# A weight stream refilled in halves of the ring: 8 MB transfers in place of 2 MB ones

## The chip, the cores and the metric

One core of a Trainium2 chip. The metric is the device time of one execution in microseconds; lower is better. All data are float32.

## The reference

The input is one image of 16 channels and 64 x 64 pixels. Four layers follow each other:

- L0 normalises the image with a 13 x 13 Gaussian blur (mean and standard deviation of the image and of a style image) and rescales it.
- L1 is a two-stage attention layer. Patches of 8 x 8 x 16 = 1024 values (64 of them) go through `Wqk_p` (1024 x 2048), `Wv_p` (1024 x 1024), attention inside each of four windows, a depthwise convolution and `Wout_p` (1024 x 1024). The four windows of 32 x 32 x 16 = 16384 values go through `Wqk_w` (1024 x 2048, on pooled values), `Wv_w` (16384 x 1024), attention between the windows, and `Wout_w` (1024 x 16384). Both results are added to the image.
- L2 is two 3 x 3 convolutions of 16 channels with a ReLU between them.
- L3 is L1 again with weights of its own.

What matters for the time: each attention layer reads 24 MB of smaller matrices (8 + 4 + 8 + 4 MB), then 64 MB of `Wv_w`, then 64 MB of `Wout_w` (MB here is 1024 x 1024 bytes). Each weight is used once, so 304 MB are read per execution.

## The kernel before

The weights are laid out as one `stream` in the order of use. The unit of use is a slot of 1 MB (2048 float32 in each of 128 partitions). The stream is read in pairs of slots (`PAIR`), that is in transfers of 2 MB with a contiguous row of 16 KB for each partition, into `ring`, which has eight such buffers (`RING`), 16 MB in all. There are 152 buffers' worth, and the last one is split into two transfers of 1 MB, so the SyncE queue (SP) issues 153 transfers for the ring.

SP issues them in order. It loads the images and the constants first (L227, L228), then eight ring buffers (L231). From then on it waits, before the transfer into buffer k, until TensorE has used the two slots that lay in it (`slots_free`, which waits on `slots_used`), and issues it (L238, L241; L244 and L245 for the two last).

TensorE (PE) runs the matmuls in one fixed order and adds one to `slots_used` after each slot. Before the first slot of a pair it waits for the pair's landing (`landed`). Its stages in each attention layer, with their lines: `Wqk_p` 8 slots (L341), `Wv_p` 4 slots (L350), turns of q, k and v (L259), `Wqk_w` 8 slots (L358) with the scores between them (L377), `Wout_p` 4 slots (L407), `Wv_w` 64 slots (L429), a short chain over ScalarE (ACT) and VectorE (DVE), and `Wout_w` 64 slots (L452). A slot is four matmuls of 512 columns for the last two stages; each shows as two instructions, so a slot is 8 instructions there. `Wout_w` is worked in groups of 8 slots (`GROUP`); after each group ACT copies the result (L579), PE turns it (L259) and DVE adds it to the image (L847). After the last group but one the finished rows are turned (L492) and stored (L594), the residual of the last rows is put into the accumulator (L499), and then the last group of 8 slots runs, whose last slot waits for the last 1 MB transfer. DVE copies the result (L868) and SP stores it (L248).

ACT fills `stage` (L567) for each 8 slots of `Wv_w`, once the 8 slots before are used. The first layer's arrays `l0_in`, `l0_sq` and `l0_blur` have memory of their own; `image_turned` is set when PE has read the last of them (L304).

Of the kernel before, what the change touches and what calls it, by code (L numbers as in the profile page):

```python
# [17 lines left out]
F32 = mybir.dt.float32  # L18
# [4 lines left out]
P = 128  # L23
# [10 lines left out]
SLOT = 2048  # L34
RING = 8
PAIR = 2
BANK = 512
# [13 lines left out]
PER_LAYER = S_OUTW + N_OUTW  # L51
TURNS = N_VW // (RING * PAIR)
GROUP = PD // P
N_BUFFERS = 2 * PER_LAYER // PAIR
assert TURNS * RING * PAIR == N_VW == N_OUTW and RING * PAIR == 2 * GROUP and N_BUFFERS % RING == 0

# [47 lines left out]

def build(nc, images, const, window_gains, small, l2w, stream, out, windows_last):
    with ExitStack() as ctx:
        def sb(name, *shape):
            return ctx.enter_context(nc.sbuf_tensor(name, list(shape), F32))

        def sem(name):  # L110
            return ctx.enter_context(nc.semaphore(name))


        ring = sb("ring", P, RING, PAIR * SLOT)
        cst = sb("cst", P, N_CONST)
# [48 lines left out]
        gains_landed, small_landed = sem("gains_landed"), sem("small_landed")  # L164
        ring_landed = [sem(f"ring_landed{i}") for i in range(RING)]
        slots_used = sem("slots_used")
        last_landed = sem("last_landed")
        last_stored = sem("last_stored")
# [30 lines left out]

        l0_in = ctx.enter_context(nc.sbuf_tensor("l0_in", [P, C, IMG], F32))  # L200
        l0_sq = ctx.enter_context(nc.sbuf_tensor("l0_sq", [P, C, IMG], F32))
        l0_blur = ctx.enter_context(nc.sbuf_tensor("l0_blur", [P, 2, 2 * BANK], F32))

        out_rows = l0_in[0:IMG].rearrange("y c x -> y (c x)")
        l0_part = l0_sq[:, :, :].rearrange("p c x -> p (c x)").rearrange("p (s n) -> p s n", s=2)

        def slot_of(L, s):

            buffer, half = divmod(L * PER_LAYER + s, PAIR)
            return ring[:, buffer % RING, half * SLOT:(half + 1) * SLOT], ring_landed[buffer % RING], buffer // RING  # L210

        def used(L, s):

            return L * PER_LAYER + s
# [10 lines left out]
        @block.sync  # L225
        def _(sp):
            sp.dma_start(l0_in[:, :, :], images).then_inc(images_landed, 16)  # L227
            sp.dma_start(cst[:, :], const).then_inc(const_landed, 16)  # L228

            for k in range(RING):  # L230
                sp.dma_start(ring[:, k, :], stream[k]).then_inc(ring_landed[k], 16)  # L231
            def slots_free(t, k):
                sp.wait_ge(slots_used, t * (RING * PAIR) + ((k + 1) * PAIR - RING * PAIR))

            with sp.Fori(1, N_BUFFERS // RING - 1) as t:
                for k in range(RING):
                    slots_free(t, k)
                    sp.dma_start(ring[:, k, :], stream[t * RING + k]).then_inc(ring_landed[k], 16)  # L238
            for k in range(RING - 1):
                slots_free(N_BUFFERS // RING - 1, k)  # L240
                sp.dma_start(ring[:, k, :], stream[N_BUFFERS - RING + k]).then_inc(ring_landed[k], 16)  # L241

            slots_free(N_BUFFERS // RING - 1, RING - 1)
            sp.dma_start(ring[:, RING - 1, 0:SLOT], stream[N_BUFFERS - 1][:, 0:SLOT]).then_inc(ring_landed[RING - 1], 16)  # L244
            sp.dma_start(ring[:, RING - 1, SLOT:], stream[N_BUFFERS - 1][:, SLOT:]).then_inc(last_landed, 16)  # L245
# [8 lines left out]
        def _(pe):  # L254
# [5 lines left out]

            def landed(L, s, turns=0):
                _, semaphore, fills = slot_of(L, s)
                if s % PAIR == 0:
                    pe.wait_ge(semaphore, turns * 16 + 16 * (fills + 1))

# [43 lines left out]
            for L in range(2):  # L309
# [26 lines left out]
                for s in range(S_QKP, S_VP):  # L336
                    landed(L, s)
                    w = slot_of(L, s)[0].rearrange("p (m h b d) -> p m b h d", m=2, b=2, d=P)
                    for m2 in range(2):
                        for b in range(2):  # L340
                            m = mm(bank[4 + m2][b * 64:b * 64 + 64, :], fl[:, s - S_QKP, :], w[:, m2, b], start=(s == S_QKP), stop=(s == S_VP - 1))  # L341
                    m.then_inc(slots_used, 1)

                for s in range(S_VP, S_QKW):
                    landed(L, s)
                    w = slot_of(L, s)[0].rearrange("p (t h b d) -> p t b h d", t=2, b=2, d=P)
                    for t in range(2):
                        kt = 2 * (s - S_VP) + t
                        for b in range(2):
                            m = mm(bank[6][b * 64:b * 64 + 64, :], fl[:, kt, :], w[:, t, b], start=(kt == 0), stop=(kt == KT - 1))  # L350
                    m.then_inc(slots_used, 1)

                def qk_of_windows(lo, hi):
                    for s in range(lo, hi):
                        landed(L, s)
                        w = slot_of(L, s)[0]
# [44 lines left out]
                for s in range(S_OUTP, S_VW):  # L401
                    landed(L, s)
                    w = slot_of(L, s)[0].rearrange("p (t f n) -> p t f n", t=2, f=2)
# [17 lines left out]
                with pe.Fori(0, TURNS) as i:  # L421
                    for k in range(RING * PAIR):
                        if k % 8 == 0:
                            pe.wait_ge(staged, i * 2 + (2 * TURNS * L + k // 8 + 1))
                        landed(L, S_VW + k, i)
                        w = slot_of(L, S_VW + k)[0].rearrange("p (j n) -> p j n", j=4)
# [17 lines left out]
                def group(i, g, onto=None):  # L444
                    for h in range(GROUP):
                        k = g * GROUP + h
                        landed(L, S_OUTW + k, i)
                        if onto is not None and h == GROUP - 1:
                            pe.wait_ge(last_landed, 16)
                        w = slot_of(L, S_OUTW + k)[0].rearrange("p (j n) -> p j n", j=4)  # L450
# [53 lines left out]
        def _(act):  # L504
# [25 lines left out]
            for L in range(2):  # L530
# [32 lines left out]
                with act.Fori(0, TURNS) as i:  # L563
                    for half in range(2):

                        act.wait_ge(slots_used, i * (RING * PAIR) + (used(L, S_VW) + 8 * half - 8))
                        sc.copy(stage[:, half, :], area[2][:, bass.ds(i * 128 + 64 * half, 64)]).then_inc(staged, 1)  # L567
# [7 lines left out]
                def copy_group(i, g):  # L575
                    act.wait_ge(slots_used, i * (RING * PAIR) + used(L, S_OUTW + GROUP * (g + 1)))
# [338 lines left out]
```

## Time and profile before

| | |
|---|---|
| time, median of 3 runs | 762.57 us (761.68 to 762.76) |
| span of the profiled execution | 760.3 us |
| outside of that span, against the median | 2.3 us |
| bytes moved in the profiled execution | 320.82 MB (10^6 bytes), 422 GB/s over the span |
| transfers into the ring | 151 of 2 MB and 2 of 1 MB |
| PE busy | 499.3 us (66%) |
| DVE busy, ACT busy | 92.3 us (12%), 38.0 us (5%) |

The profile is one execution. Its span is counted from the first to the last instruction; the time of that execution itself is not given apart from the three runs, so the 2.3 us between span and median are taken as what lies around it. Busy time of an engine is the time in which it works, and the DMA share is the mean busy share of the 16 DMA engines. In the timeline, a transfer shows through what waits for it: a PE row with "<-DMA ring<-stream" starts when a transfer has landed.

### The profile page before, as it was taken

Reading aid. Unit: us, or ns where it says so; the run is one execution under the profiler, and the core shown is the slowest. Engines: PE = TensorE matmul, PEld = TensorE weight load, DVE = VectorE, ACT = ScalarE, POOL = GpSimd, SP = SyncE. Lnnn points to the kernel's source line nnn. Section 1 sums busy time; section 2 is a strip of 40 time slices with the busy share of each in tenths; the row PEclk is TensorE's granted clock in tenths of the full one; section 3 lists DMA queues with packets and bytes.
Section 4 is the critical chain, followed back from the end, with each engine's and each line's share of the span. In section 5 each row is a group of like instructions: output and inputs, shape, how many; then the busy total and the mean of one; then the engine's idle time right before and its main releaser. Section 6 shows DMA issues by size and latency. Waiting matters only on the chain.

```text
span 760.3 us, 7405 instructions
## 1 busy us (share of the span) xinstructions
PE 499.3 (66%) x3076; PEld 143.4 (19%) x3076; DVE 92.3 (12%) x254; ACT 38.0 (5%) x79; POOL 8.8 (1%) x19
## 2 busy tenths in 40 slices
PE   6599675556556656565677979565665576666565
PEld 5234210000002211121122433000000121111121
DVE  3754400000001000000006071000000100000000
ACT  2111100000000000000001010000000000000000
POOL 2100000000000000000001000000000000000000
PEclk9589898786878777878897989978677877768789
DMA  9999999999999999999999999999999999999996
GB/s 367 427 391 431 427 428 428 429 428 428 428 428 429 428 428 428 428 428 429 428 428 427 424 428 427 431 428 428 428 428 428 428 428 428 428 430 428 429 428 280
DMA packets 22856, 320.82 MB, mean 422 GB/s; under 512 B 2569, under 2 KB 2689, under 8 KB 3257
## 3 DMA queue, kind: packets, MB, share of 16 engines
q1 hardware_dynamic: 22464, 320.04, 99.1%
q10 hardware_dynamic: 377, 0.56, 0.2%
q8 instruction: 12, 0.20, 0.1%
q14 instruction: 3, 0.02, 0.0%
HBM read 320.10 MB, written 0.49 MB: 422 GB/s over the span
## 4 chain that ended last, share of the span: by engine, by line
DMA 72%; PE 20%; DVE 6%; issue 1%; ACT 1%; SPq 0%; DVEq 0%; ACTq 0%
DMA ring<-stream 71%; PE bank L341 4%; PE bank L452 3%; PE bank L429 3%; PE bank L407 2%; DVE conv_p L772 2%; PE bank L350 2%; PE bank L259 1%; DMA cst<-const 1%; PE bank L358 1%; PE bank L476 1%; PE bank L270 0%; DVE l_sq L644 0%; PE bank L312 0%; PE bank L474 0%
## 5 line engine op out<-in xcount | busy, mean ns | idle before, releaser
L452 PE MATMUL bank<-ring,wf_t 128*32 128x512 f32 x1024 | 169.3, 797 | 99.1 <-DMA ring<-stream 93.7
L429 PE MATMUL bank<-ring,stage 128*4 128x512 f32 x1024 | 162.3, 773 | 107.5 <-DMA ring<-stream 107.5
L452 PEld LDWEIGHTS bank<-ring,wf_t 128*32 128x32 f32 x1024 | 32.7, 131 | 215.3 <-DMA ring<-stream 147.8
L429 PEld LDWEIGHTS bank<-ring,stage 128*4 128x4 f32 x1024 | 24.7, 94 | 243.3 <-DMA ring<-stream 163.6
L259 PE MATMUL bank<-cst,area 128*128 128x128 f32 (+1 forms) x234 | 38.5, 318 | 15.3 <-ACT area L579 11.6
L259 PEld LDWEIGHTS bank<-cst,area 128*128 128x128 f32 (+1 forms) x234 | 32.9, 219 | 43.9 <-ACT area L579 33.8
L847 DVE TENSOR_TENSOR image<-bank,image 128x32 f32 (+1 forms) x30 | 5.1, 194 | 278.3 <-PE bank L259 278.3
L341 PE MATMUL bank<-ring,area 128*64 128x512 f32 x128 | 33.7, 692 | 1.7 <-DVE area L728 1.7
L821 DVE COPY wv_t<-bank 128x32 f32<-128x32 f32 x2 | 0.4, 192 | 275.4 <-PE bank L259 275.4
L579 ACT COPY area<-bank 128x512 f32<-128x512 f32 x15 | 8.8, 586 | 282.3 <-PE bank L452 282.3
L407 PE MATMUL bank<-ring,area 128*64 128x512 f32 x64 | 18.0, 727 | 0.0
L341 PEld LDWEIGHTS bank<-ring,area 128*64 128x64 f32 x128 | 10.2, 159 | 24.4 <-issue 21.7
L358 PE MATMUL bank<-ring,pooled_n 128*32 128x512 f32 x128 | 14.6, 595 | 0.0
L772 DVE SCALAR_TENSOR_TENSOR conv_p<-v_pad,vec,conv_p 128x636 f32<-128x636 f32 x16 | 14.1, 881 | 0.6
L567 ACT COPY stage<-area 128x64 f32 x16 | 3.9, 242 | 205.6 <-PE bank L429 192.5
L350 PE MATMUL bank<-ring,area 128*64 128x512 f32 x64 | 14.1, 592 | 0.0
L270 PE MATMUL bank<-cst,l_in 128*128 128x128 f32 x16 | 3.7, 422 | 6.8 <-DMA cst<-const 6.8
L407 PEld LDWEIGHTS bank<-ring,area 128*64 128x64 f32 x64 | 5.3, 169 | 11.1 <-issue 11.0
L398 PE MATMUL bank<-wqk_t 128*32 128x32 f32 x4 | 0.6, 251 | 10.2 <-DVE wqk_t L787 10.2
L612 POOL TENSOR_TENSOR area<-area,vec 128x512 f32<-128x512 f32 x2 | 2.1, 1042 | 395.6 <-DVE area L703 395.6
L350 PEld LDWEIGHTS bank<-ring,area 128*64 128x64 f32 x64 | 4.5, 137 | 9.2 <-issue 9.2
L304 PE MATMUL bank<-cst,l_blur 128*64 128x64 f32 x32 | 2.0, 317 | 6.3 <-DVE l_blur L652 6.3
(193 smaller groups left out, 196.4 us busy)
## 6 DMA issues: line engine op xcount, KB each, us to landing
ring<-stream SPq DMA_DIRECT2D x151, 2048.0 KB, 35.5
ring<-stream SPq DMA_DIRECT2D x2, 1024.0 KB, 35.8
l_in<-images SPq DMA_DIRECT2D x1, 512.0 KB, 4.4
cst<-const SPq DMA_DIRECT2D x1, 461.0 KB, 5.6
area<-window_gains ACTq DMA_DIRECT2D x1, 256.0 KB, 4.6
windows_last<-area SPq DMA_DIRECT2D x1, 256.0 KB, 2.0
out<-l_in ACTq DMA_DIRECT2D x2, 112.0 KB
area<-small ACTq DMA_DIRECT2D x1, 52.0 KB
```

The lines of the kernel that those rows point to most:

```text
L259: return mm(dst, src, ident[0:rows, 0:rows], start=True, stop=True)
L341: m = mm(bank[4 + m2][b * 64:b * 64 + 64, :], fl[:, s - S_QKP, :], w[:, m2, b], start=(s == S_QKP), stop=(s == S_VP - 1))
L350: m = mm(bank[6][b * 64:b * 64 + 64, :], fl[:, kt, :], w[:, t, b], start=(kt == 0), stop=(kt == KT - 1))
L358: m = mm(bank[7][32 * j:32 * j + 32, :], pooled_n[:, s - S_QKW, :], w[:, j * BANK:(j + 1) * BANK], start=(s == S_QKW), stop=(s == S_OUTP - 1))
L407: m = mm(bank[4][f * 64:f * 64 + 64, :], a3(8, TOK)[:, h, :], w[:, t, f], start=(h == 0), stop=(h == HEADS - 1))
L429: m = mm(bank[0][32 * j:32 * j + 4, :], stage[:, k // 8, at:at + 4], w[:, j], start=False, stop=False)
L452: m = mm(bank[6 + g][32 * j:32 * j + 32, :], wf_t[:, h, :], w[:, j], start=(h == 0 and onto is None), stop=(h == GROUP - 1))
L476: mm(dst[0:32, :], taps_edge[:, n, dy, 0, :], rows(dy, -1), start=False, stop=False)
L567: sc.copy(stage[:, half, :], area[2][:, bass.ds(i * 128 + 64 * half, 64)]).then_inc(staged, 1)
L579: sc.copy(area[4 + g][:, :], bank[6 + g][:, :]).then_inc(group_copied, 1)
L772: then(v.scalar_tensor_tensor(conv_p[:, 0:159, 0:4], src, wt, conv_p[:, 0:159, 0:4], ALU.mult, ALU.add))
L847: m = v.tensor_tensor(dst, grp[:, 2 * wy:2 * wy + 2], dst, ALU.add)
```

## The change

The ring keeps its 16 MB but is filled in two halves of 8 slots, each by one transfer of 8 MB with a row of 64 KB for each partition. The weights come as two arrays, `quarters` (the 24 MB of smaller matrices of each layer, in transfers of 4 MB with rows of 32 KB) and `halves` (`Wv_w` and `Wout_w`). A further buffer `extra` of 4 MB (32 KB for each partition) takes the first and the last of a layer's six quarters; the other four go into the ring. The arrays of the first layer lie in the ring's last quarter, which is therefore filled only after `image_turned`. The halves at a layer's start and at the very end are cut: the first half of a layer comes as two transfers of 4 MB, and the last 8 slots of the kernel as 4, 2, 1 and 1 slots (`LAST_CUTS`).

```diff
-        ring = sb("ring", P, RING, PAIR * SLOT)
+        ring = sb("ring", P, TURN * SLOT)
+        extra = sb("extra", P, QUARTER * SLOT)
...
+        front = ring[:, 3 * QUARTER * SLOT:]
+        l0_in = front[:, 0:C * IMG].rearrange("p (c x) -> p c x", c=C)
...
+        out_rows = extra[0:IMG, 0:2 * BANK]
+
+        def quarter_of(j):
+
+            at = None if j in (0, N_QUARTERS - 1) else (j - 1) * QUARTER * SLOT
+            return extra[:, :] if at is None else ring[:, at:at + QUARTER * SLOT]
...
-            for k in range(RING):
-                sp.dma_start(ring[:, k, :], stream[k]).then_inc(ring_landed[k], 16)
...
+            def load_half(L, t, b, lo=0, hi=HALF):
+                sp.dma_start(ring[:, (b * HALF + lo) * SLOT:(b * HALF + hi) * SLOT],
+                             halves[t * 2 + (L * N_HALVES + b)][:, lo * SLOT:hi * SLOT]).then_inc(half_landed[b], 16)
+
+            for L in range(2):
+                load_quarter(L, 0)
+                for j in range(1, N_QUARTERS - 1):
+                    if L:
+                        sp.wait_ge(slots_used, used(L, -HALF if j < 3 else 0))
+                    elif j == N_QUARTERS - 2:
+                        sp.wait_ge(image_turned, 1)
+                    load_quarter(L, j)
+                sp.wait_ge(slots_used, used(L, QUARTER))
+                load_quarter(L, N_QUARTERS - 1)
+
+                sp.wait_ge(slots_used, used(L, 2 * QUARTER))
+                load_half(L, 0, 0, 0, QUARTER)
+                sp.wait_ge(slots_used, used(L, 3 * QUARTER))
+                load_half(L, 0, 0, QUARTER, HALF)
+                sp.wait_ge(slots_used, used(L, 5 * QUARTER))
+                load_half(L, 0, 1)
+                with sp.Fori(1, 2 * TURNS - L) as t:
+                    for b in range(2):
+                        sp.wait_ge(slots_used, t * TURN + (used(L, S_VW) + b * HALF - HALF))
+                        load_half(L, t, b)
+
+            t = 2 * TURNS - 1
+            sp.wait_ge(slots_used, used(1, S_VW) + t * TURN - HALF)
+            load_half(1, t, 0)
+            for n, landed in enumerate(last_landed):
+                lo, hi = LAST_CUTS[n], LAST_CUTS[n + 1]
+                sp.wait_ge(slots_used, used(1, S_VW) + t * TURN - HALF + hi)
+                sp.dma_start(ring[:, (HALF + lo) * SLOT:(HALF + hi) * SLOT],
+                             halves[2 * N_HALVES - 1][:, lo * SLOT:hi * SLOT]).then_inc(landed, 16)
...
-            def landed(L, s, turns=0):
-                _, semaphore, fills = slot_of(L, s)
-                if s % PAIR == 0:
-                    pe.wait_ge(semaphore, turns * 16 + 16 * (fills + 1))
+            def quarter_there(L, s):
+                if s % QUARTER == 0:
+                    pe.wait_ge(quarter_landed[s // QUARTER], 16 * (L + 1))
+
+            def half_there(L, t, b):
+
+                fills = (N_HALVES // 2 + 1, N_HALVES // 2)[b]
+                pe.wait_ge(half_landed[b], t * 16 + 16 * (L * fills + (2, 1)[b]))
...
-                        if onto is not None and h == GROUP - 1:
-                            pe.wait_ge(last_landed, 16)
+                        if onto is None and h == 0:
+                            half_there(L, i + TURNS, g)
+                        elif onto is not None and h in LAST_CUTS:
+                            pe.wait_ge(last_landed[LAST_CUTS.index(h)], 16)
...
-    nc = bacc.Bacc("TRN2", target_bir_lowering=False, num_devices=1)
+    nc = bacc.Bacc("TRN2", target_bir_lowering=False, num_devices=1, dynamic_dma_scratch_size=256)
```

The diff is cut to its core; the rest renames the addresses and waits in the PE and ACT programs to match. The arithmetic and its order on every engine stay as they were.

## Rows read from the trace of the kernel before

**Rows 1.** The page: span, busy time, the DMA lines of the 40 slices.

```profile
span 760.3 us, 7405 instructions
PE 499.3 (66%) x3076; PEld 143.4 (19%) x3076; DVE 92.3 (12%) x254; ACT 38.0 (5%) x79; POOL 8.8 (1%) x19
...
DMA  9999999999999999999999999999999999999996
GB/s 367 427 391 431 427 428 428 429 428 428 428 428 429 428 428 428 428 428 429 428 428 427 424 428 427 431 428 428 428 428 428 428 428 428 428 430 428 429 428 280
...
DMA 72%; PE 20%; DVE 6%; issue 1%; ACT 1%; SPq 0%; DVEq 0%; ACTq 0%
```

**Rows 2.** Timeline of PE in `Wv_w`: start us, us, what, [idle before <-releaser].

```profile
93.89 12.20 PE L429 MATMUL bank<-ring,stage 128*4 128x512 f32 x112
107.87 1.90 PE L429 MATMUL bank<-ring,stage 128*4 128x512 f32 x16 [1.78 <-DMA ring<-stream]
112.76 3.49 PE L429 MATMUL bank<-ring,stage 128*4 128x512 f32 x16 [2.99 <-DMA ring<-stream]
...
156.81 3.50 PE L429 MATMUL bank<-ring,stage 128*4 128x512 f32 x16 [3.00 <-DMA ring<-stream]
```

**Rows 3.** The page: DMA queue, and issues with KB and us to landing.

```profile
q1 hardware_dynamic: 22464, 320.04, 99.1%
...
ring<-stream SPq DMA_DIRECT2D x151, 2048.0 KB, 35.5
```

**Rows 4.** Windows: length, busy of PE, PEld, DVE, ACT, POOL, PEclk, DMA share, GB/s.

```profile
42.00:44.00 2.00, 2.00 (x6) 0.49 (x6) 1.90 (x8) 0.00 (x0) 0.00 (x0) 0.50 0.97 414
44.00:46.00 2.00, 2.00 (x10) 0.56 (x8) 1.93 (x8) 0.00 (x0) 0.00 (x0) 0.92 0.56 229
46.00:48.00 2.00, 2.00 (x12) 0.70 (x10) 1.90 (x8) 0.00 (x0) 0.00 (x0) 1.00 1.05 270
...
60.00:70.00 10.00, 10.00 (x90) 5.23 (x90) 2.68 (x6) 1.17 (x2) 0.00 (x0) 1.00 1.02 433
```

**Rows 5.** Timeline of SP from 36 us on: its first issues after the eight of the start.

```profile
45.14 84.74 SPq L238 DMA_DIRECT2D ring<-stream  x24
```

**Rows 6.** Timeline of PE: the first attention layer's start, then the second's.

```profile
38.32 16.92 PE L341 MATMUL bank<-ring,area 128*64 128x512 f32 x64 [0.32 <-DVE area L728]
...
382.01 3.47 PE L452 MATMUL bank<-ring,wf_t 128*32 128x512 f32 x16 [2.98 <-DMA ring<-stream]
...
410.74 16.73 PE L341 MATMUL bank<-ring,area 128*64 128x512 f32 x64 [1.38 <-DVE area L728]
427.31 7.03 PE L350 MATMUL bank<-ring,area 128*64 128x512 f32 x32
...
440.76 4.50 PE L358 MATMUL bank<-ring,pooled_n 128*32 128x512 f32 x40
...
466.04 12.20 PE L429 MATMUL bank<-ring,stage 128*4 128x512 f32 x112
479.97 0.61 PE L429 MATMUL bank<-ring,stage 128*4 128x512 f32 x4 [1.73 <-DMA ring<-stream]
```

**Rows 7.** Timeline of PE at the end.

```profile
735.45 1.92 PE L452 MATMUL bank<-ring,wf_t 128*32 128x512 f32 x16 [1.38 <-DMA ring<-stream]
...
742.58 1.90 PE L452 MATMUL bank<-ring,wf_t 128*32 128x512 f32 x16
...
751.13 4.33 PE L452 MATMUL bank<-ring,wf_t 128*32 128x512 f32 x24 [3.58 <-DMA ring<-stream]
...
756.04 1.06 PE L452 MATMUL bank<-ring,wf_t 128*32 128x512 f32 x8 [0.59 <-DMA ring<-stream]
```

**Rows 8.** Windows of the end.

```profile
752.00:753.00 1.00, 1.00 (x12) 0.34 (x8) 0.00 (x0) 0.00 (x0) 0.00 (x0) 0.50 0.79 328
...
755.00:756.00 1.00, 0.46 (x8) 0.00 (x0) 0.00 (x0) 0.00 (x0) 0.00 (x0) 1.00 0.02 8
```

**Rows 9.** The chain, in the first layer: start us, us, what.

```profile
24.73 2.00 PE bank L304 x32
```

**Rows 10.** Timeline of PE: six slots of `Wout_w` without a wait between them.

```profile
236.14 6.69 PE L452 MATMUL bank<-ring,wf_t 128*32 128x512 f32 x48 [2.64 <-DVE wf_t L837]
```

**Rows 11.** Windows over those six slots.

```profile
236.13:239.50 3.37, 3.36 (x20) 0.94 (x24) 0.00 (x0) 0.00 (x0) 0.00 (x0) 0.59 1.02 433
239.50:242.90 3.40, 3.33 (x32) 0.74 (x24) 0.00 (x0) 0.00 (x0) 0.00 (x0) 1.00 1.00 424
```

More of the change, by code:

```diff
@@ L34 @@
 SLOT = 2048
-RING = 8
-PAIR = 2
+QUARTER = 4
+HALF = 8
+TURN = 2 * HALF
 BANK = 512
@@ L51 @@
 PER_LAYER = S_OUTW + N_OUTW
-TURNS = N_VW // (RING * PAIR)
+TURNS = N_VW // TURN
 GROUP = PD // P
-N_BUFFERS = 2 * PER_LAYER // PAIR
-assert TURNS * RING * PAIR == N_VW == N_OUTW and RING * PAIR == 2 * GROUP and N_BUFFERS % RING == 0
+N_QUARTERS = S_VW // QUARTER
+N_HALVES = (N_VW + N_OUTW) // HALF
+assert TURNS * TURN == N_VW == N_OUTW and HALF == GROUP and N_QUARTERS == TURN // QUARTER + 2
+LAST_CUTS = (0, 4, 6, 7, 8)
 CONST = {}
@@ L102, in constants, with build @@
     return c
-def build(nc, images, const, window_gains, small, l2w, stream, out, windows_last):
+def build(nc, images, const, window_gains, small, l2w, quarters, halves, out, windows_last):
     with ExitStack() as ctx:
@@ L164, in build @@
         gains_landed, small_landed = sem("gains_landed"), sem("small_landed")
-        ring_landed = [sem(f"ring_landed{i}") for i in range(RING)]
+        quarter_landed = [sem(f"quarter_landed{j}") for j in range(N_QUARTERS)]
+        half_landed = [sem(f"half_landed{b}") for b in range(2)]
         slots_used = sem("slots_used")
-        last_landed = sem("last_landed")
+        last_landed = [sem(f"last_landed{n}") for n in range(len(LAST_CUTS) - 1)]
         last_stored = sem("last_stored")
@@ L228, in _ @@
             sp.dma_start(cst[:, :], const).then_inc(const_landed, 16)
-            for k in range(RING):
-                sp.dma_start(ring[:, k, :], stream[k]).then_inc(ring_landed[k], 16)
[L232 to L245, printed above, removed]
+            def load_quarter(L, j):
+                sp.dma_start(quarter_of(j), quarters[L * N_QUARTERS + j]).then_inc(quarter_landed[j], 16)
@@ L336, in _ @@
                 for s in range(S_QKP, S_VP):
-                    landed(L, s)
-                    w = slot_of(L, s)[0].rearrange("p (m h b d) -> p m b h d", m=2, b=2, d=P)
+                    quarter_there(L, s)
+                    w = slot_of(s).rearrange("p (m h b d) -> p m b h d", m=2, b=2, d=P)
                     for m2 in range(2):
@@ L344, in _ @@
                 for s in range(S_VP, S_QKW):
-                    landed(L, s)
-                    w = slot_of(L, s)[0].rearrange("p (t h b d) -> p t b h d", t=2, b=2, d=P)
+                    quarter_there(L, s)
+                    w = slot_of(s).rearrange("p (t h b d) -> p t b h d", t=2, b=2, d=P)
                     for t in range(2):
@@ L354, in qk_of_windows @@
                     for s in range(lo, hi):
-                        landed(L, s)
-                        w = slot_of(L, s)[0]
+                        quarter_there(L, s)
+                        w = slot_of(s)
                         for j in range(4):
@@ L401, in _ @@
                 for s in range(S_OUTP, S_VW):
-                    landed(L, s)
-                    w = slot_of(L, s)[0].rearrange("p (t f n) -> p t f n", t=2, f=2)
+                    quarter_there(L, s)
+                    w = slot_of(s).rearrange("p (t f n) -> p t f n", t=2, f=2)
                     for t in range(2):
@@ L421, in _ @@
                 with pe.Fori(0, TURNS) as i:
-                    for k in range(RING * PAIR):
-                        if k % 8 == 0:
+                    for k in range(TURN):
+                        if k % HALF == 0:
                             pe.wait_ge(staged, i * 2 + (2 * TURNS * L + k // 8 + 1))
-                        landed(L, S_VW + k, i)
-                        w = slot_of(L, S_VW + k)[0].rearrange("p (j n) -> p j n", j=4)
+                            half_there(L, i, k // HALF)
+                        w = slot_of(S_VW + k).rearrange("p (j n) -> p j n", j=4)
                         for j in range(4):
@@ L564, in _ @@
                     for half in range(2):
-                        act.wait_ge(slots_used, i * (RING * PAIR) + (used(L, S_VW) + 8 * half - 8))
+                        act.wait_ge(slots_used, i * TURN + (used(L, S_VW) + 8 * half - 8))
                         sc.copy(stage[:, half, :], area[2][:, bass.ds(i * 128 + 64 * half, 64)]).then_inc(staged, 1)
@@ L575, in copy_group @@
                 def copy_group(i, g):
-                    act.wait_ge(slots_used, i * (RING * PAIR) + used(L, S_OUTW + GROUP * (g + 1)))
+                    act.wait_ge(slots_used, i * TURN + used(L, S_OUTW + GROUP * (g + 1)))
                     act.wait_ge(group_added, i * 2 + added(L, g - 1))
@@ L888, in dram @@
         return nc.dram_tensor(name, a.shape, mybir.dt.from_np(a.dtype), kind="ExternalInput").ap()
-    gains, smalls, pieces = [], [], []
+    gains, smalls, first, rest = [], [], [], []
     for n in ("L1_conv", "L3_conv"):
@@ L895 @@
         smalls += [v[k].reshape(P, 9).T for k in ("conv_p_w", "conv_w_w")]
-        pieces += [in_tiles(arr(f"{n}_{k}"), PAIR * SLOT // arr(f"{n}_{k}").shape[1]) for k in ("Wqk_p", "Wv_p", "Wqk_w", "Wout_p", "Wv_w")]
+        first += [in_tiles(arr(f"{n}_{k}"), QUARTER * SLOT // arr(f"{n}_{k}").shape[1]) for k in ("Wqk_p", "Wv_p", "Wqk_w", "Wout_p")]
+        rest += [in_tiles(arr(f"{n}_Wv_w"), HALF * SLOT // PD)]
         out_w = arr(f"{n}_Wout_w")
-        pieces += [in_tiles(out_w[:, at:at + SLOT], PAIR) for at in range(0, WD, SLOT)]
-    stream = dram("stream", np.concatenate(pieces))
+        rest += [in_tiles(out_w[:, at:at + SLOT], HALF) for at in range(0, WD, SLOT)]
+    quarters, halves = dram("quarters", np.concatenate(first)), dram("halves", np.concatenate(rest))
     l2w = np.concatenate([arr(f"L2_conv_{k}").transpose(1, 2, 3, 0).reshape(C, 9 * C) for k in ("w1", "w2")]
@@ L909 @@
     windows_last = nc.dram_tensor("windows_last", (P, WIN * C), F32, kind="ExternalOutput").ap()
-    build(nc, images, const, window_gains, small, l2, stream, out, windows_last)
+    build(nc, images, const, window_gains, small, l2, quarters, halves, out, windows_last)
     r = run_bass_kernel_spmd(nc, [arrays], core_ids=[0]).results[0]
```

20 lines of the change are left out of this document (9 added, 11 removed).

## The prediction

> **What bounds the kernel now.** First the page's shares and slices [rows 1]: no compute engine is near full (PE 66%), while the DMA engines are at nine tenths or more in every slice but the last, at 428 GB/s. The chain puts 72% on DMA, nearly all of it on the ring's transfers. Then the PE timeline in `Wv_w` [rows 2]: the rows start 4.89 us apart, each released by a landing, ten of them from 107.87 to 156.81, so one 2 MB transfer every 4.894 us, or 2,097,152 B / 4.894 us = 428.5 GB/s. Between landings PE works 1.9 to 3.5 us and waits. A transfer takes 35.5 us from issue to landing [rows 3], which is 7.25 such steps: the wait is a queue seven transfers deep, not latency. 320.82 MB at 428.5 GB/s are 748.7 us of the 760.3. So the reader should look for only two things: whether the stream runs at a better rate, and where it runs dry.
>
> It runs dry once. The windows at 42 to 48 us show 414, 229 and 270 GB/s [rows 4]: all 16 MB had landed, and SP's first further issue stands at 45.14 [rows 5], when PE had used the first two slots of `Wqk_p` [rows 6]. Missing are 2 x (14.5 + 199.5 + 158.5) = 745 KB, that is 1.7 us. The rate is back only about 2 us after the issue. I use that 2 us below as the lead that an issue needs.
>
> **The change, part by part.**
>
> *Fewer, wider transfers.* Before there are 153 into the ring. After: 12 quarters, 4 of 4 MB for the two cut first halves, 15 halves in the first layer, 14 in the second, 4 cuts at the end: 49. 104 fall away. What does one cost when the queue is never empty? The trace has one direct comparison: the last 2 MB came as two transfers, and from the landing at 751.13 to the one at 756.04 are 4.91 us [rows 7], against 4.894 for one of 2 MB [rows 2]. That is 0.016 us for one transfer more. It is likely too low, since some DMA engines were already done by then (328 GB/s at 752 us, 8 at 755) [rows 8]. The other end: the best rate of a stretch of 10 us is 433 GB/s [rows 4], at which 2 MB take 4.843 us. If all of the difference is fixed cost, it is 0.051 us a transfer. Rows of 64 KB in place of 16 KB can only save part of the same difference. Bounds 1.7 and 5.3 us for 104 transfers, and nothing if the cadence goes by bytes alone. I take 0.040, nearer the upper end because the lower one was measured with idle engines: **-4.2 us**.
>
> A page prices this quite otherwise. The Trainium skill's page "SBUF — State Buffer" (section "The DMA setup-cost knee") gives each transfer a roughly fixed 2 us and advises the largest single transfer; exposed, 104 of them would be 208 us, but the trace does not agree that it is exposed: transfers land 4.894 us apart with seven queued. The page "DMA: Bandwidth & Descriptors" (section "Where 436 GB/s comes from") gives a ceiling of 435 GB/s; at it 2 MB take 4.819 us, and an estimate from that page would be 0.075 us a transfer or 7.8 us in all.
>
> *20 MB ahead at the start.* `extra` lets SP queue five quarters before PE uses anything. The fourth ring quarter waits for `image_turned`, at 26.7 us [rows 9]; the stream arrives there after 16 MB, which is later than 42 us [rows 4]. So the wait is free. Quarter 5 needs four slots used: 38.32 plus 10.1 (two slots at the slow pace until 45.14, then 1.68 each) is 48.4 us, and 20 MB last until about 57. The dry spell goes: **-1.7 us**.
>
> *Later releases.* Space now comes back eight slots at a time. In steady state a half lands every 19.6 us. PE needs for eight slots: six took 6.69 us from a cold start [rows 10], the first part at a granted clock of 0.59, the rest at 1.00 [rows 11]; plus two at 0.87 gives 8.4 us. After `Wout_w` groups some 3 us of copying and turning follow. All of that lies under the other half's 19.6 us, even at the 1.2 GHz level throughout (13.6 us). ACT's waits for `stage` go by slots used, as before. SP's queue has nothing behind its waits but later ring transfers.
>
> The two layer starts need a count. Let T be the landing of the last slots before the second layer (382.01) [rows 6]. PE then has eight slots to run, not two: 8.4 against 3.5 us, so all that follows is 4.9 later, and `Wqk_p` starts at T + 28.7 + 4.9 = T + 33.6. From T the queue holds 40 MB up to the second half of `Wv_w`; one MB takes 2.447 us. Each issue must come 2 us before the queue ends:
>
> - quarter 5: four slots used at T + 43.7, needed T + 46.9
> - first half's two pieces: eight used at T + 50.2, needed T + 56.7; twelve at T + 57.2, needed T + 66.5
> - second half: twenty used at T + 68.1, needed T + 76.3
> - next half: `Wv_w` starts 55.3 after `Wqk_p` and eight slots take 7.0 (fourteen took 12.20) [rows 6], so used at T + 95.9, needed T + 97.9 - 2 = T + 95.9
>
> The last is late by nothing for the DMA engine that ends last. But the engines end up to 3 us apart [rows 8], and the early ones would stand idle that long. Cost 0 to 3 us, **+1.5** taken. In the first layer the same 40 MB landed at 107.87 with the dry spell in it, so 106.1 without; eight slots are used at 93.89 + 7.0 = 100.9 [rows 2], needed at 104.1: hidden, with 3.2 us to spare for the last engine and about none for the first. If PE ran at the slow level there, 6.6 us would be added at each place.
>
> *The end.* With E the last landing, the last half but one lands at E - 19.6. Eight slots 8.4, then the turns and the residual as before (737.4 to 742.58, 5.2) [rows 7], so PE is free for the last eight slots at E - 6.0. Four take 3.5, then two 1.7, then one 0.9 (their landings at E - 9.8, - 4.9, - 2.4 are earlier): the last slot starts at E + 0.1: **+0.1**, up to 5 if the eight slots ran at the slow level.
>
> *The rest.* The constants and images are issued first as before. Other waits and renamed addresses cost nothing: PE has slack of a third of the span. The smaller scratch argument frees space and moves no work.
>
> Sum: -4.2 - 1.7 + 1.5 + 0.1 = -4.3 us. The profiled span of 760.3 becomes 756.0; with the 2.3 us outside it, or from the median 762.57, that is **758.3 us**.
>
> **The rivals.**
>
> - *By bytes alone.* The cadence does not depend on size, since the DMA share is already 0.99 to 1.01 with no visible gap. Against it: 4.91 for two pieces. Then only the stalls count: 762.57 - 1.7 + 1.5 = 762.4, no change that shows. Chance 0.17.
> - *The full 433 GB/s, and no new stall.* 320.82 MB at 433 are 740.9 us, 7.8 less; with the dry spell gone 753.1. For it: many short windows reach it [rows 4, 11]. Against it: no stretch of 20 us but one or two does [rows 1]. Chance 0.12.
> - *The halves starve the stream.* Place: SP's wait for the first half of `Wv_w` in either layer. It decides once that half is used over 6 us later than counted, so that the stall passes the 5.9 us won. Eight slots at the slow level add 6.6, in both layers 13; with the lower bound for transfers: 762.57 - 1.7 - 1.7 + 1.5 + 6.6 = 767.3, or about 764 where it is half so bad. Against it: PE came into `Wv_w` dense and ran 14 slots in 12.20 us. Chance 0.13.
> - *Wide rows read slower.* The 16 engines would read at places four times further apart. Nothing in the trace speaks to it; 1% of the rate is 7.5 us, and with the other terms 762.57 + 7.5 - 1.7 + 1.5 = 769.9, or 766 at half a per cent. Chance 0.08. "DMA: Bandwidth & Descriptors" of the Trainium skill (section "Latency and other measured facts") has copies of the same tile shape lose 3% at a row pitch of 512 KiB, and more above; here the pitch is 64 KiB, and no run here shows such a loss yet.
>
> **How the numbers follow.** The forecast has 0.50. 0.2% (1.5 us) is about what a measurement of this kernel can tell from no change. Faster by more: the forecast, the full rate and a small part of the bytes-alone case, 0.66. Within it: most of the bytes-alone case and a mild starving, 0.19. Slower: 0.15. The likeliest case alone spans 755.7 (5.3 for transfers, no new stall: 762.57 - 5.3 - 1.7 + 0.1) to 760.7 (1.7 for transfers, 1.5 more of stall at the start or the end). The range reaches from 753.0, the full rate, to 764.0, past bytes alone and into mild starving; what is left out is the bulk of the two slow cases and a little below.
>
> **What the profile would show.** The packets of the ring's queue, 22,464 before [rows 3], should fall to well under half, or the rows are cut up again and only the transfers count. Halves should land 19.43 us apart (4 x 4.894 - 3 x 0.05) if the fixed cost is 0.05, 19.58 if there is none. 42 to 48 us should show 428 GB/s. Some 95 us after the last landing of the first attention layer a window may fall under 400; far more than 3 us of it makes the starving rival right. The last PE slot should start within 0.3 us of the last landing. The prediction is wrong if the cadence of halves is 19.6 or more, or if SP's wait for PE ends after the queue is empty more than once.

## The result and the profile after

| | before | after |
|---|---|---|
| time, median | 762.18 us (4 runs, 761.68 to 762.76) | 754.73 us (4 runs, 753.38 to 755.45) |
| ratio | | 0.9898, interval 0.9885 to 0.9911 |
| span of the profiled execution | 760.3 us | 751.6 us |

The change makes the kernel 1.0% faster. The time lies inside the range forecast, 753.0 to 764.0, but the gain is 7.45 us where 4.3 were forecast. The sign was right and the size was not.

The page of the changed kernel: DMA slices, packets, queue, chain.

```profile
span 751.6 us, 6984 instructions
PE 452.6 (60%) x3076; PEld 145.0 (19%) x3076; DVE 91.8 (12%) x254; ACT 38.0 (5%) x79; POOL 8.8 (1%) x19
...
GB/s 377 432 431 432 451 423 433 429 443 439 419 429 443 443 419 429 436 446 429 420 428 435 425 433 440 416 443 401 446 443 443 398 446 440 443 422 426 443 417 283
...
q1 hardware_dynamic: 7488, 320.03, 98.8%
...
DMA 59%; PE 35%; DVE 5%; ACT 1%; issue 1%; SPq 0%; DVEq 0%; ACTq 0%
```

The ring's queue has 7,488 packets instead of 22,464 [rows 3]. The fall of 14,976 is 104 transfers x 16 engines x 9: for each transfer that is gone, each engine moves its eight rows and one packet more (run 2 shows that one alone). So the rows of 64 KB do go as one packet each, as those of 16 KB did. The slices no longer stand at a steady 428 as in [rows 1]; between the first and the last they swing from 398 to 451. That goes with the longer packets, which fall into one slice or the next: in run 2, which has the same 49 transfers and packets of 16 KB, all but one of the slices stand at 426 to 431 again. The cadence of landings is the better meter. This is PE in `Wout_w` of the first layer, a row for each half:

```profile
240.79 9.98 PE L489 MATMUL bank<-ring,wf_t 128*32 128x512 f32 x64 [5.31 <-DMA ring<-halves]
260.14 8.84 PE L489 MATMUL bank<-ring,wf_t 128*32 128x512 f32 x64 [7.42 <-DMA ring<-halves]
...
337.53 7.68 PE L489 MATMUL bank<-ring,wf_t 128*32 128x512 f32 x48 [8.56 <-DMA ring<-halves]
```

Five halves in 337.53 - 240.79 = 96.74 us are 19.35 us for 8 MB, or 4.837 us for 2 MB, where before one took 4.894 [rows 2]. That is 433.6 GB/s as a mean over 97 us, where before 433 was only the best window of 10 us [rows 4]. The prediction said that it would be wrong from a cadence of 19.6 us on, and expected 19.43 to 19.58; the cadence came out below both.

The second layer's start, PE's timeline:

```profile
376.23 8.83 PE L489 MATMUL bank<-ring,wf_t 128*32 128x512 f32 x64 [7.43 <-DMA ring<-halves]
...
410.54 8.76 PE L378 MATMUL bank<-extra,area 128*64 128x512 f32 x32 [1.58 <-DVE area L765]
...
464.17 7.05 PE L466 MATMUL bank<-ring,stage 128*4 128x512 f32 x64
474.67 8.75 PE L466 MATMUL bank<-ring,stage 128*4 128x512 f32 x64 [3.45 <-DMA ring<-halves]
494.30 9.50 PE L466 MATMUL bank<-ring,stage 128*4 128x512 f32 x64 [10.88 <-DMA ring<-halves]
```

and DMA there, by windows:

```profile
468.00:470.00 2.00, 2.00 (x24) 0.54 (x20) 0.00 (x0) 0.00 (x0) 0.00 (x0) 1.00 0.83 360
470.00:472.00 2.00, 1.22 (x12) 0.11 (x4) 0.00 (x0) 0.24 (x1) 0.00 (x0) 1.00 0.61 262
```

The first eight slots of `Wv_w` are used at 464.17 + 7.05 = 471.2, and the DMA share has fallen to 0.61 by then: the new dry spell stands where the prediction put it. For the DMA engine that lands last it cost 494.30 - 474.67 - 19.35 = 0.3 us in this execution.

The end, PE's timeline and the window after which the DMA engines are nearly idle:

```profile
726.76 9.35 PE L489 MATMUL bank<-ring,wf_t 128*32 128x512 f32 x64 [8.64 <-DMA ring<-halves]
...
741.32 7.05 PE L489 MATMUL bank<-ring,wf_t 128*32 128x512 f32 x64
```
```profile
746.00:747.00 1.00, 1.00 (x16) 0.36 (x12) 0.00 (x0) 0.00 (x0) 0.00 (x0) 1.00 0.04 16
```

PE runs all eight last slots without one wait, to 748.4, while the ring's last bytes are in before 747. In [rows 7] its last slot waited for its landing and ran 1.06 us. So PE is about half a microsecond late here; the prediction allowed 0.3.

### The profile page after: what moved, and what is told of

It is laid out like the page before. It is cut to its first block, busy times and chain, and to the rows that moved or that the text cites. A ratio compares the mean times of both kernels' runs of the same rounds, so it can differ in the third digit from the quotient of the medians.

```text
span 751.6 us, 6984 instructions
## 1 busy us (share of the span) xinstructions
PE 452.6 (60%) x3076; PEld 145.0 (19%) x3076; DVE 91.8 (12%) x254; ACT 38.0 (5%) x79; POOL 8.8 (1%) x19
## 3 DMA queue, kind: packets, MB, share of 16 engines
q1 hardware_dynamic: 7488, 320.03, 98.8%
## 4 chain that ended last, share of the span: by engine, by line
DMA 59%; PE 35%; DVE 5%; ACT 1%; issue 1%; SPq 0%; DVEq 0%; ACTq 0%
DMA ring<-halves 58%; PE bank L489 11%; PE bank L466 10%; PE bank L378 4%; PE bank L387 2%; PE bank L395 1%; PE bank L292 1%; PE bank L444 1%; DVE conv_p L809 1%; DMA cst<-const 1%; PE bank L513 1%; PE bank L358 1%; PE bank L307 1%; DVE ring L681 0%; PE bank L349 0%
## 5 line engine op out<-in xcount | busy, mean ns | idle before, releaser
L466 PE MATMUL bank<-ring,stage 128*4 128x512 f32 x1024 | 142.2, 718 | 130.5 <-DMA ring<-halves 130.5
L489 PE MATMUL bank<-ring,wf_t 128*32 128x512 f32 x1024 | 148.1, 743 | 114.7 <-DMA ring<-halves 114.7
L489 PEld LDWEIGHTS bank<-ring,wf_t 128*32 128x32 f32 x1024 | 36.1, 133 | 215.0 <-DMA ring<-halves 117.7
L292 PE MATMUL bank<-cst,area 128*128 128x128 f32 (+1 forms) x234 | 33.0, 286 | 15.5 <-ACT area L616 11.8
L292 PEld LDWEIGHTS bank<-cst,area 128*128 128x128 f32 (+1 forms) x234 | 28.1, 191 | 35.5 <-ACT area L616 25.4
L378 PE MATMUL bank<-extra,area 128*64 128x512 f32 x64 | 17.4, 704 | 1.9 <-DVE area L765 1.9
L444 PE MATMUL bank<-extra,area 128*64 128x512 f32 x64 | 18.4, 741 | 0.0
L378 PE MATMUL bank<-ring,area 128*64 128x512 f32 x64 | 14.1, 592 | 0.0
L387 PE MATMUL bank<-ring,area 128*64 128x512 f32 x64 | 14.1, 592 | 0.0
L307 PE MATMUL bank<-cst,ring 128*128 128x128 f32 x16 | 3.8, 431 | 6.8 <-DMA cst<-const 6.8
L378 PEld LDWEIGHTS bank<-extra,area 128*64 128x64 f32 x64 | 5.1, 163 | 13.4 <-issue 10.5
L444 PEld LDWEIGHTS bank<-extra,area 128*64 128x64 f32 x64 | 5.3, 170 | 11.5 <-issue 11.3
L358 PE MATMUL bank<-area,cst 128*128 128x512 f32 x4 | 4.1, 1140 | 4.3 <-ACT area L570 4.3
```

The lines of the kernel that those rows point to most:

```text
L292: return mm(dst, src, ident[0:rows, 0:rows], start=True, stop=True)
L307: m = mm(bank[pair // 4][:, pair % 4 * P:pair % 4 * P + P], l0_in[:, 2 * pair:2 * pair + 2, :].rearrange("p c x -> p (c x)"), cc("blur_y") ...
L358: mm(bank[0][:, :], ones, area[1][:, :], start=True, stop=True).then_inc(var_sums, 1)
```

## Experiments

All are edits of the changed kernel, except that the fifth is the changed kernel itself. Ratios are against the kernel before on the same chip. Runs 1 to 4 were taken on one chip, 5 to 8 on a second, 9 and 10 on a third, so medians of different groups are compared by their ratios too.

### 1. Same ring, pieces of 2 MB

```diff
-                sp.dma_start(ring[:, (b * HALF + lo) * SLOT:(b * HALF + hi) * SLOT],
+                for c in range(lo, hi, PIECE):          # PIECE = 2, waits for 16 per piece
+                    sp.dma_start(ring[:, (b * HALF + c) * SLOT:(b * HALF + c + PIECE) * SLOT],
...
```

The quarters and the last cuts are issued in pieces in the same way, 153 transfers in all.

> The changed kernel with its ring, buffers and waits for space as they are, but every large transfer issued as pieces of 2 MB (16 KB rows), 153 in all instead of 49. Theory A (a fixed cost of about 0.073 us per transfer with its eight rows per engine, read from the changed kernel's landings: 9.71 us for 4 MB, 19.35 us for 8 MB, against 4.894 us for 2 MB): landings 4.894 us apart, 104 x 0.073 = 7.6 us slower than the changed kernel, about 762.3 us, the same as the kernel before within 1 us. Rival (the gain came from the ring's structure, more data queued ahead and the dry spell gone, or from the layout in HBM): the cadence stays at 4.838 us per 2 MB and the time within 1.5 us of 754.7.

Measured: 761.50 us (760.83 to 763.13), ratio 0.9993 (0.9983 to 1.0002). The whole gain is gone, although the ring, the extra buffer, the deeper start and the layout in HBM are those of the changed kernel. Landings, from PE's timeline:

```profile
243.27 9.59 PE L495 MATMUL bank<-ring,wf_t 128*32 128x512 f32 x64 [5.77 <-DMA ring<-halves]
...
341.19 4.13 PE L495 MATMUL bank<-ring,wf_t 128*32 128x512 f32 x24 [7.96 <-DMA ring<-halves]
```

97.92 / 5 = 19.58 us for 8 MB, four times the 4.894 of [rows 2]. The rival falls. This run moves the number of transfers and the width of rows together, so it does not say which of them counts.

### 2. Same 49 transfers, rows of 16 KB

```diff
-    quarters, halves = dram("quarters", np.concatenate(first)), dram("halves", np.concatenate(rest))
+    def cut(w):
+        return w.reshape(w.shape[0], P, -1, ROW).transpose(0, 2, 1, 3)      # ROW = 2 * SLOT
+    quarters, halves = dram("quarters", cut(np.concatenate(first))), dram("halves", cut(np.concatenate(rest)))
...
+                sp.dma_start(ring[:, (b * HALF + lo) * SLOT:(b * HALF + hi) * SLOT].rearrange("p (c n) -> p c n", n=ROW),
+                             halves[t * 2 + (L * N_HALVES + b)][lo // 2:hi // 2].rearrange("c p n -> p c n")).then_inc(half_landed[b], 16)
```

> The changed kernel with the same 49 transfers, but each of them moves rows of 16 KB (four rows per partition for 8 MB, two for 4 MB), laid out in HBM as the kernel before had them. Theory A1 (the fixed cost is paid per row that an engine moves): the cost comes back, 8 MB take about 19.35 + 24 x 0.009 = 19.57 us and the time is about 762 us. Theory A2 (it is paid per transfer, at its completion): 19.35 us and 754.7 us. A split of the cost shows as something between: with half of it per row, about 758.5 us.

Measured: 761.85 us (760.76 to 762.36), ratio 0.9993 (0.9983 to 1.0003), the same as the first run. The queue's packets and two landings five halves apart:

```profile
q1 hardware_dynamic: 20800, 320.03, 99.0%
```
```profile
243.09 10.01 PE L494 MATMUL bank<-ring,wf_t 128*32 128x512 f32 x64 [5.39 <-DMA ring<-halves]
...
340.97 4.57 PE L494 MATMUL bank<-ring,wf_t 128*32 128x512 f32 x24 [9.21 <-DMA ring<-halves]
```

97.88 / 5 = 19.58 us. With a third of the transfers and the same rows nothing is won: the first and second run differ by 104 transfers and by nothing in the cadence. So the fixed cost is paid per row that an engine moves, and not per transfer. The two also differ in layout: the first takes pieces of 16 KB out of rows of 64 KB, the second reads contiguously. That a cost of the transfers and a gain of the layout cancel is ruled out by the kernel before, which has the 153 transfers of the one and the contiguous rows of the other, and the same cadence (4 x 4.894 = 19.58 us). The packets of the two runs, 22,464 and 20,800, differ by 104 x 16, one for each transfer and engine; these packets show no cost, the rows do.

### 3. Same ring, pieces of 1 MB

The edit is that of the first run with `PIECE = 1`.

> As the first run, but in pieces of 1 MB (8 KB rows), about 305 transfers. Theory A: 2.41 + 0.073 = 2.483 us for each MB, so 256 x 0.073 = 18.7 us slower than the changed kernel, about 773.4 us. Rival (the cadence goes by bytes and only structure counts): within 1.5 us of 754.7.

Measured: 772.23 us (772.09 to 772.50), ratio 1.0132 (1.0115 to 1.0149).

```profile
246.71 9.28 PE L495 MATMUL bank<-ring,wf_t 128*32 128x512 f32 x64 [6.23 <-DMA ring<-halves]
...
326.35 8.72 PE L495 MATMUL bank<-ring,wf_t 128*32 128x512 f32 x64 [9.52 <-DMA ring<-halves]
```

79.64 / 4 = 19.91 us for 8 MB in 64 rows per engine. Twice the rows cost a further 0.33 us a half, and 10.7 us in all.

### 4. The dry spell at the start put back

```diff
-                        sp.wait_ge(image_turned, 1)
+                        sp.wait_ge(slots_used, 2)
```

> The changed kernel, but in the first attention layer SP holds back the fifth quarter until PE has used two slots, so that 16 MB are queued ahead as before, and the stream runs dry near 45 us. By the prediction's term the dry spell costs 1.7 us on the mean of the DMA engines: 756.4 us. If only the engine that ends last counts, 1.2 to 1.7 us. Rival (the dry spell was made up elsewhere): no change, 754.7 us.

Measured: 756.27 us (755.90 to 756.87), 1.5 us above the first measurement of the changed kernel and 0.9 above run 5's median (1.7 and 0.8 by the ratios). Its window, and that of the changed kernel:

```profile
38.00:48.00 10.00, 9.68 (x37) 2.97 (x38) 9.26 (x32) 1.98 (x4) 0.00 (x0) 0.81 0.95 381
```
```profile
38.00:48.00 10.00, 9.69 (x37) 2.97 (x38) 9.24 (x33) 1.99 (x4) 0.00 (x0) 0.81 0.97 417
```

36 GB/s over 10 us are 360 KB or 0.8 us, less than the 1.7 of [rows 4]. The edit does not bring back the whole spell: SP's late issue stands at 43.95, and at 45.14 in [rows 5].

```profile
43.95 0.33 SPq L243 DMA_DIRECT2D ring<-quarters  x1
```

Nor is the start all that differs in this run's trace. It has the longest stall of all at the refill near 471 us:

```profile
474.72 7.05 PE L466 MATMUL bank<-ring,stage 128*4 128x512 f32 x64 [0.45 <-DMA ring<-halves]
497.57 9.53 PE L466 MATMUL bank<-ring,stage 128*4 128x512 f32 x64 [15.80 <-DMA ring<-halves]
```

The step is 22.85 us, 3.5 above the cadence. So a cost of the start between 0.8 and 1.7 us agrees with the times, and this run does not say where in between.

### 5. The changed kernel again

No edit.

> The changed kernel itself, unedited, on the same chip as the next three, so that they can be set against it: 754.7 us, 1.0% below the kernel before.

Measured: 755.36 us (753.25 to 755.51), ratio 0.9910 (0.9895 to 0.9925). It is the base for runs 6 to 8. The profiled execution is the fastest of the four (753.25); the other three, at 755.3 to 755.5, left no trace.

### 6. Rows of 32 KB in the halves

Each half is issued as two transfers of 4 MB once the whole half is free.

```diff
+                for c in range(lo, hi, QUARTER):
+                    sp.dma_start(ring[:, (b * HALF + c) * SLOT:(b * HALF + c + QUARTER) * SLOT],
```

> The changed kernel, but each half issued as two transfers of 4 MB with rows of 32 KB, when the whole half is free: 16 rows per engine and half in place of 8. Theory (about 0.0096 us for each row that an engine moves, from 19.58 us with 32 rows, 19.35 with 8): 8 MB every 19.43 us, 29 x 8 x 0.0096 = 2.2 us slower than the changed kernel, about 757.0 us. Rival (a threshold: rows wider than 16 KB are all as good, or only those of 64 KB are): 754.7 or 762 us.

Measured: 755.27 us (755.01 to 757.36), ratio 0.9910 (0.9897 to 0.9924).

```profile
241.58 9.71 PE L489 MATMUL bank<-ring,wf_t 128*32 128x512 f32 x64 [5.57 <-DMA ring<-halves]
...
338.74 6.78 PE L489 MATMUL bank<-ring,wf_t 128*32 128x512 f32 x44 [9.08 <-DMA ring<-halves]
...
467.54 7.05 PE L466 MATMUL bank<-ring,stage 128*4 128x512 f32 x64
476.17 7.05 PE L466 MATMUL bank<-ring,stage 128*4 128x512 f32 x64 [1.58 <-DMA ring<-halves]
497.88 9.54 PE L466 MATMUL bank<-ring,stage 128*4 128x512 f32 x64 [14.67 <-DMA ring<-halves]
```

The cadence is as expected, 97.16 / 5 = 19.43 us, so there is no threshold in width. The time is not: the lowest and highest are 1.8 us above those of run 5, but the median is the same, where 2.2 us more were expected. The 2.2 us are shown in the cadence alone. The same rows show how long the new dry spell can be: PE starts `Wv_w` at 467.54, and the step from 476.17 to 497.88 is 21.71 us, 2.3 above the cadence.

### 7. Two cuts more

Both cuts: the first refill of the ring's lower half in two pieces, the first issued four slots earlier, and the last half but one in two pieces that PE waits for one by one.

```diff
+                sp.wait_ge(slots_used, used(L, S_VW) + QUARTER)
+                load_half(L, 1, 0, 0, QUARTER)
+                sp.wait_ge(slots_used, used(L, S_VW) + HALF)
+                load_half(L, 1, 0, QUARTER, HALF)
...
-            load_half(1, t, 0)
+            for n, landed in enumerate(early_landed):
+                lo, hi = n * QUARTER, (n + 1) * QUARTER
+                sp.dma_start(ring[:, lo * SLOT:hi * SLOT], halves[2 * N_HALVES - 2][:, lo * SLOT:hi * SLOT]).then_inc(landed, 16)
```

> The changed kernel with two halves cut into two transfers of 4 MB: in each layer the first refill of the ring's lower half, of which the first piece is issued four slots earlier, and at the end the last half but one, so that PE starts on it 9.7 us earlier. It removes the new dry spell near 471 us (2.0 us for the DMA engines that end first, 0.3 us for the one that ends last) and the 0.5 us by which PE starts the last slot late. It adds 24 rows per engine, 0.2 us. If only the last engine counts: 0.6 us less than the changed kernel. If the mean of the engines counts, about 1.5 us less. Rival (neither stands on the path): no difference.

Measured: 752.94 us (752.59 to 753.74), ratio 0.9879 (0.9864 to 0.9894), 2.4 us below run 5, more than either expectation (0.6 and 1.5). It has the lowest median here, though run 9 is within its interval, and its time spreads over 1.2 us instead of 2.3.

### 8. The last half in two pieces only

```diff
-LAST_CUTS = (0, 4, 6, 7, 8)
+LAST_CUTS = (0, 4, 8)
```

> The changed kernel with its last half as two transfers of 4 MB instead of four of 4, 2, 1 and 1 MB. PE can start the last four slots only when all of them have landed, about 746.65 us in the profile, and needs 3.45 us for them, so it ends near 750.1 instead of 748.4: 1.7 us slower than the changed kernel. Rival (the last slots are not on the path): no difference or 0.15 us less.

Measured: 757.06 us (756.26 to 758.23), ratio 0.9937 (0.9923 to 0.9950), 1.7 us above run 5.

```profile
747.60 3.64 PE L489 MATMUL bank<-ring,wf_t 128*32 128x512 f32 x32 [1.38 <-DMA ring<-halves]
```

PE waits for the last 4 MB and then needs 3.64 us for four slots. What is worth cutting is what PE has to do behind the last landing.

### 9. The cut of the refill alone

The first part of run 7's diff.

> The changed kernel with the first refill of the ring's lower half alone cut into two transfers of 4 MB, the first issued four slots earlier (one of the two cuts of the seventh run). In the traces so far the half that follows lands 30.1 to 30.3 us after PE starts Wv_w in the second layer, whenever that is, so the whole stream waits for PE there: 0.3 us where PE starts at 464.2, 3 us where it starts at 467.5. Theory: with the cut that wait is gone or under 0.3 us, the time is 0.5 to 2 us below the changed kernel's (753.3 to 754.8) and spreads less, under 1.3 us from lowest to highest. Rival (the seventh run's gain came from the end): 754.7 to 755.4 us with the spread of 2 us kept.

Measured: 753.35 us (752.81 to 753.82), ratio 0.9886 (0.9870 to 0.9903), with a spread of 1.0 us. By the medians that is 2.0 us below run 5 and 1.4 below the first measurement of the changed kernel, by the ratios 1.8 and 0.9.

```profile
465.43 7.05 PE L473 MATMUL bank<-ring,stage 128*4 128x512 f32 x64
474.94 7.05 PE L473 MATMUL bank<-ring,stage 128*4 128x512 f32 x64 [2.46 <-DMA ring<-halves]
494.36 5.98 PE L473 MATMUL bank<-ring,stage 128*4 128x512 f32 x40 [12.37 <-DMA ring<-halves]
```

PE starts `Wv_w` 1.3 us later than in the changed kernel's profile, and still the next half lands 28.9 us after that, not 30.1, and 19.42 after the one before, which is the cadence of a half in two pieces. The stall is gone from the windows too, here beside run 6's:

```profile
472.00:478.00 6.00, 3.54 (x40) 0.81 (x36) 0.00 (x0) 0.25 (x1) 0.00 (x0) 1.00 0.98 421
```
```profile
472.00:478.00 6.00, 4.42 (x47) 1.00 (x40) 0.00 (x0) 0.24 (x1) 0.00 (x0) 1.00 0.67 240
```

With this refill cut (runs 7 and 9) all eight executions took at most 753.82 us; without it (the first measurement, runs 5 and 10) nine of twelve took 754.16 us or more, and the other three reach the low times as well.

### 10. The cut at the end alone

The second part of run 7's diff.

> The changed kernel with only the last half but one cut into two transfers of 4 MB (the other cut of the seventh run). Theory: PE is free 3 us earlier for the last eight slots and starts the last slot when it lands, 0.5 us less than the changed kernel, 754.2 to 754.9 us, with its spread of 2 us kept. Rival (the end is where the seventh run's 2.4 us came from): about 753 us.

Measured: 754.89 us (752.86 to 755.45), ratio 0.9908 (0.9891 to 0.9925), which is run 5's 0.9910 and not below the first measurement's 0.9898; the spread is kept (2.6 us).

```profile
737.69 5.52 PE L496 MATMUL bank<-ring,wf_t 128*32 128x512 f32 x48
744.35 1.06 PE L496 MATMUL bank<-ring,wf_t 128*32 128x512 f32 x8 [1.14 <-DMA ring<-halves]
746.80 1.07 PE L496 MATMUL bank<-ring,wf_t 128*32 128x512 f32 x8 [1.38 <-DMA ring<-halves]
```

PE is free 3.6 us earlier and again waits for the last landing, at 746.80. The profiled execution took 752.86 us, and those of the two measurements of the changed kernel, whose PE came to `Wv_w` within 0.3 us of this one's, 753.38 and 753.25. That the end costs about 0.5 us is read from the traces; the medians do not show it.

## Why the prediction was right or wrong

**What bounds the kernel: right.** The stream of weights bounds it before and after. The cadence goes with the rows in every run, and the times follow it to within the 2 us by which executions of one kernel differ (run 6).

**The step that failed: the fixed cost per transfer.** That the stream would gain by a fixed cost beside its bytes was right. The prediction took "0.040, nearer the upper end" for each of 104 transfers, 4.2 us, with 0.051 as the upper bound; the runs show about 0.080 for each transfer's eight rows, 8.3 us. Two things were off.

- *The size.* The cadence went from 4.894 to 4.837 us for 2 MB. With rows of 64, 32, 16 and 8 KB (8, 16, 32 and 64 rows per engine and half), 8 MB take 19.35, 19.43, 19.58 and 19.91 us. The steps give 0.010, 0.009 and 0.010 us a row. The kernel before moves 152 x 8 + 8 = 1,224 rows of the ring per engine, the changed one 49 x 8 = 392. 832 rows at 0.010 are 8.3 us, an estimate from the cadences. The profiled executions of runs 1 and 2 took 8.3 and 8.65 us more than that of the changed kernel. Their medians are only 6.1 to 7.1 us above its two, most likely because its other executions lose more at the refill than the profiled one.
- *What it is paid for.* The prediction counted transfers and held that wide rows "can only save part of the same difference". Run 2 shows that the rows carry all of it and the 104 transfers nothing that the cadence or the time shows. This did not move the number: a transfer has eight rows per engine in either kernel, so 104 transfers and 832 rows are the same count. It would mislead whoever gathers rows of unchanged width into fewer transfers.

Both bounds came from rows that could not carry them. The 4.91 us of [rows 7] was taken while the DMA engines ran out of work [rows 8], so it understated the cost of eight more rows (0.016 us, where 0.08 is right). The 433 GB/s of [rows 4] was a window of 10 us at the old rate, not a ceiling. Without the rows' cost, 8 MB would take 19.35 - 0.08 = 19.27 us, or 435.3 GB/s, as an estimate. The ceiling of 435 GB/s in the Trainium skill's page "DMA: Bandwidth & Descriptors" (section "Where 436 GB/s comes from") agrees with this, and the 7.8 us that the prediction worked out from it, per transfer as well, and left aside, was the better value. The fixed 2 us a transfer of the Trainium skill's page "SBUF — State Buffer" (section "The DMA setup-cost knee") is nowhere exposed in a queue that is never empty; runs 1 and 2 agree on that.

**The dry spell at the start: right in kind, its size open.** It is gone in the trace (417 GB/s at 38 to 48 us). Run 4 puts back a shorter one and loses 0.8 us in the window and 0.8 to 1.7 us in the time, against 1.7 forecast. At 42 to 44 us PE's granted clock was 1.00 in that run and 0.50 in [rows 4]:

```profile
42.00:44.00 2.00, 2.00 (x12) 0.70 (x10) 1.93 (x8) 0.00 (x0) 0.00 (x0) 1.00 1.22 524
```

So the first two slots were used 1.2 us earlier, by which its spell is shorter, and 1.7 us for the whole one is not refuted.

**The later releases: right in place, and mostly in size.** Forecast was 0 to 3 us at the first refill in the second layer, with 1.5 taken. At the engine that lands last the traces show 0.3 us (changed kernel), 2.3 us (run 6) and 3.5 us (run 4), and cutting that refill gives 0.9 to 2.0 us of the median. That the price changes from execution to execution was not in the prediction. From the last landing of the first layer to `Wv_w` PE needed 87.9 us in the changed kernel's profile (376.23 to 464.17) and 90.0 in run 6's (377.59 to 467.54), with stretches at the 1.2 GHz level that were longer in run 6. First the changed kernel, then run 6:

```profile
410.00:415.00 5.00, 4.46 (x14) 1.43 (x16) 3.50 (x11) 1.70 (x3) 0.00 (x0) 0.61 1.00 424
415.00:420.00 5.00, 5.00 (x28) 1.55 (x24) 0.00 (x0) 0.00 (x0) 0.00 (x0) 1.00 0.99 426
```
```profile
377.59 9.97 PE L489 MATMUL bank<-ring,wf_t 128*32 128x512 f32 x64 [8.03 <-DMA ring<-halves]
```
```profile
410.00:415.00 5.00, 3.42 (x10) 1.39 (x10) 4.16 (x13) 1.34 (x4) 0.00 (x0) 0.50 0.98 419
415.00:420.00 5.00, 5.00 (x20) 1.46 (x18) 1.42 (x3) 0.71 (x2) 0.00 (x0) 0.74 0.99 418
```

The stream waits for PE at this one place, so what PE loses by the clock becomes time. That the executions at 755.3 to 755.5 us lost their 2 us in the same way is not shown by a trace; runs 7 and 9, where they do not occur, speak for it.

**The end: right in kind.** Forecast 0.1 us, read from the trace 0.5: the eight slots took 9.35 us, not 8.4. The 8.4 came from one stretch, [rows 10], whose first 3.4 us had a granted clock of 0.59 [rows 11]; here the first 3.3 us had 0.50 and the next three 0.77:

```profile
726.70:730.00 3.30, 3.24 (x16) 0.79 (x20) 0.00 (x0) 0.00 (x0) 0.00 (x0) 0.50 1.10 477
730.00:733.00 3.00, 3.00 (x28) 0.83 (x24) 0.00 (x0) 0.00 (x0) 0.00 (x0) 0.77 0.81 350
```

**The sum.** -8.3 (rows) - 1 to 1.7 (start) + 0.3 to 2.3 (refill) + 0.5 (end) lies between -9.2 and -6.5; measured -7.45. The rows gave 4.1 us more than forecast and the other terms took about one of it back. The range held the result only because its lower end was set by the full-rate rival, at a chance of 0.12, and not by the likeliest case, whose 755.7 to 760.7 the result misses. Run 1 checks the rest without the rows: ring, start, refill and end together are worth -0.5 us (interval -1.3 to +0.2).

**The rivals.** The full rate was right about the rate, by luck, since its reason was short windows at the old rate, and wrong that no stall would come. Bytes alone and wide rows reading slower are refuted by the cadences. The halves starve the stream, but mildly, and only in one of the two places.

## What to carry to other kernels

When a queue of transfers never runs empty, count the rows that each DMA engine moves: that count times about 0.01 us here is what the stream loses, and gathering the same rows into fewer transfers wins nothing. Coarser buffers bought for wider rows give some of it back where the consumer starts late, so cut just the refill that follows such a start and the transfers that the last work waits for. And before taking an upper bound from a good window, ask whether anything in it was different from the rest; if not, it is scatter and bounds nothing.

## What the runs showed of the hardware

- A row of 64 KB per partition moves as one packet, and each row costs an engine about 0.010 us beyond its bytes, at 8, 16, 32 and 64 KB alike: 19.91, 19.58, 19.43, 19.35 us for 8 MB.
- A transfer on top of others in the same queue costs nothing measurable: 153 against 49 with the same rows, 761.50 and 761.85 us, and 19.58 us for 8 MB in both.
- The level at which PE's clock is granted becomes time where the stream waits for PE: 464.17 us at `Wv_w` and a stall of 0.3 us in one execution, 467.54 and 2.3 us in another (run 6's kernel). The spread of the times is weaker evidence: the changed kernel's four lie over 2.3 us and run 9's over 1.0, but those of the kernel before lie over 1.0, 1.8 and 2.6 us in the three groups of runs.
